# The first step of an attention kernel: its first weights in two pieces, and another order on all engines

## The reference

```python
x = x + _L0_xattn_ref(_layernorm(x), ctx_1024, Wq, Wk, Wv, Wo, gq, gk)
# inside: 16 heads of 128
q = rmsnorm(x @ Wq, gq); k = rmsnorm(ctx @ Wk, gk); v = ctx @ Wv
attn = softmax(q k^T / sqrt(128)); out = (attn @ v) @ Wo
```

## Time and profile before

| | |
|---|---|
| times of three runs | 2042.27, 2046.19, 2047.24 us (median 2046.19) |
| profiled execution | 2046.22 us, span of its instructions 2044.4 us |
| PE busy | 1992.8 us, 97% of the span |
| DVE, ACT, POOL busy | 1288.2, 794.4, 530.1 us |
| granted TensorE clock, mean | 0.991 |

### The profile page before, as it was taken

How to read it: one execution, slowest core, us unless ns; L and a number is a source line. 1 busy time by engine, 2 the same in 40 slices (tenths; PEclk the granted TensorE clock), 3 DMA queues, 4 the chain that set the end, 5 groups by cost and what they waited for, 6 DMA issues and landing times. The chain is left out here.

```text
span 2044.4 us, 33384 instructions
## 1 busy us (share of the span) xinstructions
PE 1992.8 (97%) x12656; PEld 1646.3 (81%) x12656; DVE 1288.2 (63%) x2265; ACT 794.4 (39%) x2371; POOL 530.1 (26%) x579
## 2 busy tenths in 40 slices
PE   6999999999999999999999999999999999999998
PEld 5888888888888887878888777777787788888886
DVE  5555555665555555342435488888757877887787
ACT  5555555655555543211112355454432222122211
POOL 3222222321223324410103243332210222222231
PEclk9999999999999999999999899999999999999999
DMA  6100000200011112120104100000112355554555
GB/s 231 51 5 5 8 5 10 78 28 29 29 57 52 50 32 82 52 83 0 62 29 128 59 20 21 18 21 16 45 52 72 134 181 185 190 189 158 188 174 185
DMA packets 76487, 154.16 MB, mean 75 GB/s; under 512 B 8816, under 2 KB 31088, under 8 KB 76400
## 3 DMA queue, kind: packets, MB, share of 16 engines
q0 software_dynamic: 23712, 87.04, 12.8%
q1 hardware_dynamic: 52688, 65.97, 9.8%
HBM read 136.21 MB, written 16.78 MB: 75 GB/s over the span
## 5 line engine op out<-in xcount | busy, mean ns | idle before, releaser
L2351 POOL DMA_INDIRECT m_ring<-in_table,m_row x128 | 126.3, 987 | 391.2 <-DVE l_x_all L2464 284.8
L48 PE MATMUL four_banks<-l_yT_hi,m_hi 128*128 128x512 f32 x512 | 199.4, 390 | 0.0
L48 PE MATMUL four_banks<-l_yT_lo,m_hi 128*128 128x512 f32 x512 | 199.2, 389 | 0.0
L1121 DVE TENSOR_SCALAR f_relu<-bank,f_b 128x512 f32<-128x512 f32 x64 | 47.9, 749 | 165.1 <-ACT f_h_hi L1064 165.1
L511 ACT ACTIVATE prob<-four_banks,mx,rms 128x128 f32<-128x128 f32 x256 | 114.0, 463 | 92.1 <-DVE mx L645 92.1
L1064 ACT ACTIVATE f_h_hi<-bank,f_b 128x512 fp32r<-128x512 f32 x64 | 44.1, 689 | 262.9 <-PE bank L48 262.9
L289 POOL TENSOR_TENSOR rms<-ssq,constants 128x8 f32<-128x8 f32 x64 | 13.0, 204 | 435.9 <-ACT junk L496 263.8
L2328 ACT ACTIVATE m_act_of<-m_dot,l_ln_y 128x2 f32<-128x2 f32 x64 | 18.9, 296 | 241.4 <-DVE m_junk L2454 241.4
L48 PEld LDWEIGHTS four_banks<-l_yT_hi,m_hi 128*128 128x128 f32 x512 | 96.1, 188 | 20.2 <-issue 0.2
L48 PEld LDWEIGHTS four_banks<-l_yT_lo,m_hi 128*128 128x128 f32 x512 | 96.1, 188 | 19.8
L48 PE MATMUL four_banks<-wo_hi,oT_hi 128*128 128x512 f32 x256 | 106.4, 416 | 4.7 <-DVE oT_lo L660 4.7
(11 more groups left out here) (304 smaller groups left out, 5584.3 us busy)
## 6 DMA issues: line engine op xcount, KB each, us to landing
f_stage<-in_w POOLq DMA_DIRECT2D x14, 512.0 KB, 4.5
f_x_in<-x SPq DMA_DIRECT2D x18, 256.0 KB, 2.9
ctx_in<-in_ctxT SPq DMA_DIRECT2D x32, 128.0 KB, 2.5
x_in<-in_x SPq DMA_DIRECT2D x16, 256.0 KB, 2.6
x<-xres SPq DMA_DIRECT2D x16, 256.0 KB, 2.0
x<-l_x_all SPq DMA_DIRECT2D x16, 256.0 KB, 2.0
m_stage<-in_gate SPq DMA_DIRECT2D x8, 512.0 KB, 6.2
m_stage<-in_up SPq DMA_DIRECT2D x8, 512.0 KB, 7.3
```

Of the source, the lines that this page charges most:

```text
L48: mm = pe.matmul(out, st, mv, start=first and n == 0, stop=last and n == len(terms) - 1)
L1121: dve.tensor_scalar(relu[m % 2][:], bank[HB[m % 2]][:], b12[:, layer, m:m + 1], 0.0, ALU.add, ALU.max).then_inc(S["relu_ready"], 1)
L2351: pool.indirect_dma_start(ring[slot][:], None, table, bass.IndirectOffsetOnAxis(ap=row[:, tile_of(g), k:k + 1], axis=0)).then_inc(S[f"got{ ...
```

## The change

Weights wq0 are fetched in two pieces of 512 KB (input rows 0 to 255, then 256 to 511) with a semaphore each, and are rounded and subtracted as two pieces of 128x1024; PE starts the first product of queries(0, 0) when piece 0 is split and waits for piece 1 in the middle. SP issues the identity ahead of ctx; it waits for the second piece of wq0 before xres piece 1, gq and gk, and for wk before xres piece 2. POOL sets its constants after two fetches and puts the rest of the fetches between its first roots and splits. PE begins with 24 products of a zeroed 128x128 block with itself, into a bank that nothing reads before it is written again. On ACT and DVE the splits of wq1, wv0 and wv1 go behind other work of step 0, and on DVE statistics(1) goes behind the second piece of wq0, and the splits of wk0 and wk1 behind the product of gq and gk.

```diff
+    FIRST_CUTS = {"wq0": 2}
+    def cuts(n, h):
+        return h + FIRST_CUTS.get(n, 1)
+    def first_queries(part, i):
+        return wqp[0][part][:, 2 * i:2 * i + 2, :].rearrange("p k w -> p (k w)"), stage[0][:, 1024 * i:1024 * (i + 1)]
+    def first_hi(act, i):
+        out, raw = first_queries(0, i)
+        act.wait_ge(S[("wq0_staged", "wq0_rest_staged")[i]], 16)
+        act.activation(out, raw, ACT.Copy).then_inc(S["wq0_hi"], 1)
+    def first_lo(dve, i):
+        out, raw = first_queries(1, i)
+        dve.wait_ge(S["wq0_hi"], i + 1)
+        dve.tensor_tensor(out, raw, first_queries(0, i)[0], ALU.subtract).then_inc(S["wq0_cut"], 1)
...
@@ sync, step FIRST
                 load_res(0)
+                sp.dma_start(ident[:], ident_in).then_inc(S["ident_loaded"], 16)
                 load_ctx(0)
-                sp.dma_start(ident[:], ident_in).then_inc(S["ident_loaded"], 16)
+                sp.wait_ge(S["wq0_rest_staged"], 16)
                 load_res(1)
                 sp.dma_start(gqk[:, 0:1], gq).then_inc(S["g_loaded"], 16)
                 sp.dma_start(gqk[:, 1:2], gk).then_inc(S["g_loaded"], 16)
+                sp.wait_ge(S["wk_staged"], 16)
                 load_res(2)
@@ gpsimd, step FIRST
-                for n in ("wq0", "wk", "wq1", "wv", "wo0", "wo1"):
-                    fetch(n, 0)
+                for i, what in enumerate(("wq0_staged", "wq0_rest_staged")):
+                    rows = wq[0].rearrange("(k p) w -> p k w", p=P)[:, 2 * i:2 * i + 2, 0:G * D]
+                    pool.dma_start(first_queries(0, i)[1].rearrange("p (k w) -> p k w", k=2), rows).then_inc(S[what], 16)
                 for i, value in enumerate((D * EPS, -0.5, EPS)):
                     pool.memset(constants[:, i, :], value).then_inc(S["set"], 1)
-                pool.wait_ge(S["set"], 3)
+                pool.memset(q_sb[0][:, 0:P], 0.0).then_inc(S["set"], 1)
+                fetch("wk", 0)
+                fetch("wq1", 0)
+                pool.wait_ge(S["set"], 4)
                 root(0)
+                fetch("wv", 0)
                 split_ctx(0)
+                fetch("wo0", 0)
+                fetch("wo1", 0)
                 root(1)
@@ tensor
+            if isinstance(s, int) and s == 0 and g == 0:
+                pe.wait_ge(S["wq0_cut"], 1)
...
+                product(pe, bank[7][:], pairs[0:2], last=False)
+                pe.wait_ge(S["wq0_cut"], 2)
+                product(pe, bank[7][:], pairs[2:4], first=False).then_inc(S["q_made0"], 1)
...
+        def keep_busy():
+            pe.wait_ge(S["set"], 4)
+            for _ in range(24):
+                pe.matmul(bank[6][:, 0:P], q_sb[0][:, 0:P], q_sb[0][:, 0:P], start=True, stop=True)
...
+            if now == FIRST:
+                keep_busy()
@@ scalar
+            if now == 0:
+                split_hi(act, "wq1", 0)
             if there(s):
                 square_k(s, 0)
                 copy_qT(s, 0)
+            if now == 0:
+                split_hi(act, "wv0", 0)
+                split_hi(act, "wv1", 0)
...
             if now == FIRST:
                 split_ctx(0)
-                split_hi(act, "wq0", 0)
+                first_hi(act, 0)
             if there(s + 1):
                 split_xT(s + 1)
             if now == FIRST:
-                for n in ("wk0", "wk1", "wq1", "wv0", "wv1"):
-                    split_hi(act, n, 0)
+                first_hi(act, 1)
+                split_hi(act, "wk0", 0)
+                split_hi(act, "wk1", 0)
@@ vector
-            if now == FIRST:
-                statistics(1)
             if now == 0:
-                split_lo(dve, "wv0", 0)
-                split_lo(dve, "wv1", 0)
+                split_lo(dve, "wq1", 0)
...
             if now == FIRST:
-                split_lo(dve, "wq0", 0)
+                first_lo(dve, 0)
             if there(s + 1):
                 split_xT(s + 1)
             if now == FIRST:
-                for n in ("wk0", "wk1", "wq1"):
-                    split_lo(dve, n, 0)
+                first_lo(dve, 1)
+                statistics(1)
             if there(s):
                 copy_kT(s, 0)
+            if now == 0:
+                split_lo(dve, "wv0", 0)
+                split_lo(dve, "wv1", 0)
...
                 then(dve.scalar_tensor_tensor(gqk[:, 2:3], gqk[:, 0:1], float(D) ** 0.5, gqk[:, 1:2], ALU.mult, ALU.mult))
+                split_lo(dve, "wk0", 0)
+                split_lo(dve, "wk1", 0)
```

More of the change, by code:

```diff
@@ L135, in l0_attention @@
         g_loaded stats_ready ln_eps ln_ready xn_ready xT_turned xT_hi xT_lo ctx_hi ctx_split set eps_added0 eps_added1 stored
-        s_turn y_begun y_ready y_added wq0_staged wv_staged wk_staged wq1_staged wo0_staged wo1_staged""".split()
+        s_turn y_begun y_ready y_added wq0_staged wq0_rest_staged wv_staged wk_staged wq1_staged wo0_staged wo1_staged""".split()
     names += [f"{n}{g}" for g in range(2) for n in """q_made k_made v_made q_copied v_copied q_squared k_squared
@@ L186, in split_hi @@
         act.activation(home(n, 0), staged(n, h), ACT.Copy).then_inc(S[f"{n}_hi"], 1)
+    FIRST_CUTS = {"wq0": 2}
[11 more added lines that the diff above has]
+        dve.tensor_tensor(out, raw, first_queries(0, i)[0], ALU.subtract).then_inc(S["wq0_cut"], 1)
     def split_lo(engine, n, h):
-        engine.wait_ge(S[f"{n}_hi"], h + 1)
+        engine.wait_ge(S[f"{n}_hi"], cuts(n, h))
         engine.tensor_tensor(home(n, 1), staged(n, h), home(n, 0), ALU.subtract).then_inc(S[f"{n}_cut"], 1)
@@ L194, in new_weights @@
         if isinstance(s, int) and s % NB == 0:
-            pe.wait_ge(S[f"{n}_cut"], s // NB + 1)
+            pe.wait_ge(S[f"{n}_cut"], cuts(n, s // NB))
     FIRST, LOOP0, END0, LOOP1, END1, LAST = -1, 3, NB - 2, NB + 2, AHEAD_FROM, STEPS + 1
@@ L316, in step @@
                 split_lo(pool, "wq0", 1)
-                fetch("wq1", 1, after=[("wq0", 2)])
+                fetch("wq1", 1, after=[("wq0", 3)])
                 split_lo(pool, "wv0", 1)
@@ L327, in step @@
             if now == 0:
-                fetch("wq0", 1, after=[("wq0", 1)])
+                fetch("wq0", 1, after=[("wq0", 2)])
                 fetch("wv", 1, after=[("wk0", 1), ("wk1", 1)])
@@ L351, in queries @@
                 pe.wait_ge(*at("xT_lo", s))
-            new_weights(pe, s, f"wq{g}")
+            if isinstance(s, int) and s == 0 and g == 0:
+                pe.wait_ge(S["wq0_cut"], 1)
+            else:
+                new_weights(pe, s, f"wq{g}")
             pairs = [((xTp[0][:, k, :], xTp[1][:, k, :]), (wqp[g][0][:, k, :], wqp[g][1][:, k, :])) for k in range(KD)]
+            if isinstance(s, int) and s == 0 and g == 0:
+                product(pe, bank[7][:], pairs[0:2], last=False)
+                pe.wait_ge(S["wq0_cut"], 2)
+                product(pe, bank[7][:], pairs[2:4], first=False).then_inc(S["q_made0"], 1)
+                return
             product(pe, bank[(7, 3)[g]][:], pairs).then_inc(S[f"q_made{g}"], 1)
```

## The result

| | before | changed |
|---|---|---|
| median (range), 18 runs each | 2043.74 (2039.21 to 2048.33) us | 2046.53 (2044.78 to 2052.15) us |
| profiled execution | 2046.22 us | 2046.27 us |
| its span | 2044.4 us | 2044.0 us |
| PE busy | 1992.8 us | 1997.9 us |

The ratio is 1.0018, 95% interval 1.0011 to 1.0026.

What follows compares the result with a forecast made beforehand. PE, busy from 47 us for 700 us, was taken to bound the kernel, so only its earlier work there counts: 4.4 - 0.35 = 4.05, rounded to 4.1 us, from 2046.22 to 2042.1 us; range 2038.8 to 2045.9.

Steps and rivals of the forecast that it cites:

- Zeros, identity, first product: Begin of PE: zeros end at 10.6, queries(0, 0) at 15.7 in place of 20.2, 4.5 us earlier.
- What is late next: Small loads behind the first product: xres piece 1 lands at 13.8, gk at 17.1, keys(0, 0) starts at 18.5.
- the second rival: Small loads as slow as before: gk lands at 21.4, only 0.4 us gained, 2045.8 us; chance 0.17.
- xres piece 2 hidden: Load lands at 21.2, DVE asks for it at 22.8: hidden by wq1's split, up to 1.6 us.
- PE in step 0: Low clock taken for keys(0, 0); queries(0, 1) starts at 23.5 against 27.88, 4.4 us earlier.
- 0.7 us in the good direction alone: Rival that the clock stays high before keys: 4.75 us gained in place of 4.05, 2041.4 us; chance 0.2.
- wv behind kT: DVE's wv splits after copy_kT: values(0, 0) loses 0.35 us waiting for wv0 lo, the rest is hidden.
- No later stage gives it back by rows, since PE is full for 700 us behind: Stages after 47 us: the 4.05 us gained at the begin, rounded to 4.1, reaches the end.
- The slow small loads: Same as the second rival: gk takes 10.8 us from its issue, 0.4 us gained; chance 0.17.
- The slower rival: Zeros at PE's begin do not raise the clock: 0.6 us slower, 2046.8 us; chance 0.06.

Runs made afterwards that it cites:

- e4: The changed kernel again, word for word, beside runs of before: 2047.10 us, ratio 1.0011.
- r1: A single traced execution of the unaltered changed kernel: 2046.31 us.
- r2: Another single traced execution of the unaltered changed kernel: 2047.17 us.
- e1: The changed kernel without the 24 products of zeros: 2044.09 us, ratio to before 0.9995.
- e3: The changed kernel with DVE's wk splits moved ahead of statistics(1) and of the product of gq and gk: 2041.24 us, ratio to before 0.9981.
- e2: The changed kernel without SP's two waits, for wq0's second piece and for wk: 2042.35 us, ratio to before 0.9986.
- e8: The changed kernel with unread products of the identity put into PE's waits at the begin: 2042.92 us, ratio to before 0.9992.
- e10: The changed kernel with 6 zero products of 512 columns in place of 24 of 128: 2044.28 us, ratio to before 1.0008.
- e6: e3 without the products of zeros: 2043.32 us, ratio to before 0.9988.
- e12: e10 with POOL's memset of the zeros cut into seven, so six more POOL instructions: 2044.92 us, ratio to before 0.9994.
- e13: e3 with wq1 hi early, no SP wait for wk, 6 wide zero products, 8 identity products before scores, POOL's memset cut into seven: 2041.06 us, ratio 0.9982.
- e9: e3 with wq1 hi rounded early, no SP wait for wk, and unread identity products in PE's waits: 2042.32 us, ratio to before 0.9993.

## Why the prediction was wrong

The changed kernel against before, by means over four traces each: M 1.1 us earlier, 1.5 us lost at 904, 0.8 at 1899: 1.2 us slower, where 4.05 faster were forecast. So of the 5.3 us between forecast and traces, 3.0 are missing at the begin and 2.3 are lost behind it. The profiled spans give 1.7 slower (mean 2044.2 against 2042.5), 0.5 more, about half of it at the clock's steps near 1159 and 1476 and half at the wait near 1696. The medians gave 2.8, the repeat in e4 1.7; what is above 1.2 is not tied to the change by any trace.

- **Zeros, identity, first product: right.** Zeros end at 10.7 (forecast 10.6), ctx lands at 8.2 (9.0), products 12.54 to 15.68 (12.65 to 15.7); in r1 and r2 the zeros end at 11.8, within the bounds. But e1 shows that this term is worth nothing in the changed kernel, since the landings decide behind it.
- **"What is late next": the sizes failed.** xres piece 1 was put at 13.8 and landed at 16.5; gk at 17.1, and landed at 19.4. Both were worked out as distances to another landing (and twice the 2.0 us behind the issue at 9.5 give 13.5, not 13.8). Counted from its issue, gk was given 6.5 us, where rows 7 had 10.8; here it was 9.0, and 7.0 for xres piece 1. That was between the forecast and the second rival. Keys started at 21.03 against 18.5: most of what is missing at the begin. The "Queues, rings and completion order" rule of the Trainium skill's page "DMA: Bandwidth & Descriptors", cited for 17.1, did not save the small load here: turn by turn or not, 512 bytes took 9.0 us behind 256 KB of SP's own queue and beside the weights.
- **xres piece 2 hidden: right, by luck.** DVE took it at 24.67 without a wait, but it landed at 23.5 (12.10 + 11.4), not at 21.2. At 22.8, where the forecast had DVE ask for it, DVE would have waited 0.7 us; it was gk that made DVE late. e3, which has no wait for gk there, waited 1.18 us for it.
- **PE in step 0: mixed.** The low clock at the keys came, as chosen. That it could reach most of keys(0, 1) as well was in no case; it did in two of four traces, and these took 0.8 us more from keys to queries(0, 1) by means. The rule of the Trainium skill's page "TensorE: Matmul & The Clock Gate" cited for a level that differs from run to run agrees with this: the low stretch ended at 24.0, 24.5, 26.5 and 26.5 us. I had given it 0.7 us in the good direction alone.
- **wv behind kT: right.** Values started 1.13 us behind the scores against 0.88: 0.25 lost, forecast 0.35.
- **"No later stage gives it back by rows, since PE is full for 700 us behind": failed.** PE full until 747 says nothing of 904 and 1899. And two instruction streams got longer at the begin (96 instructions on PE, two on POOL), which the part by part did not price at all: it counted the zeros' time, and not their place in the stream. The runs show 1.5 us at 904 and 0.8 at 1899 in its place. This is the step that turned a small gain into a loss.
- **The rivals.** The slow small loads (0.4 us, 0.17) were the nearest for the begin. The slower rival was the wrong one: the zeros did raise the clock. The loss of 2.3 us by fetches was in none.

What is shown: the splits behind the two landings (e3, with e2), the clock behind the waits (e8), PE's fetch (e10, e1, e6 against the eight) and POOL's (e12, e13). Not settled: the 0.7 us at 904 in e8 and e13, why e10's executions fall in two groups, and the level of the clock near 760, 1159 and 1476 us. With the wait near 1696 it moves the rest of before alone between 1994.1 and 1997.8 us, more than the 2.3 us lost at 904 and 1899, so no single span decides between two of these kernels.

## What to carry to other kernels

A small load that others wait for is to be costed from its issue, with the duration that a like one had beside the same busy queue, and what stands behind its wait in the order of an engine should be moved ahead where it doesn't need it: that was worth 2.6 to 4.4 us at M here (41.78 in one trace, against 44.34 to 46.19). Instructions added at the begin of an engine's stream move its later instruction fetches to other places of the program: in all 20 traces the fetch that hit the load here came at the same count of PE's instructions, within 32. Compare the traces at stages far behind the edit before a loss there is called noise, and write filler work in few wide instructions.

## What the runs showed of the hardware

- A 16 KB piece of PE's instructions fetched beside a 256 KB load of an engine's input went with 1.3 to 1.8 us more waiting for that load, in 8 of 8 profiles; moving the piece removed it in e10. Two profiles (e8, e13) waited 0.7 us more without a piece inside the load.
- The pieces come by count of instructions: the one that hit the load at 9879 to 9911 of PE's matmuls and weight loads, the one that hit the gathers at 790 or 791 of POOL's instructions, in 20 of 20 traces.
- With a fetch of POOL's instructions (8 KB) on a pair of gathers, the second took 1.70 us to issue in place of 0.93, and PE, 15 us later, lost 0.2 to 1.4 us (13 of 13 traces, none in the other 7).
- Half a kilobyte took 9.0 us to land beside a full weights' queue, and 10.6 when it was issued early (e2).
- The same program had PE at 1.2 GHz behind its waits until 24.0, 24.5 or 26.5 us in four traces; the two later ones took 0.8 us more from the keys to queries(0, 1). With small products in PE's waits, the traces of e8 and e9 show no such stretch.
